# Row maxima as rows of the q stack, sent on ScalarE's DMA queue, and z transposed a step ahead, in a cross-attention block

## What is computed

```python
x = layer_norm(hidden_states, ln1_w, ln1_b)
q = (x @ q_w + q_b).reshape(B, LQ, H, HD).transpose(0, 2, 1, 3)
k = (encoder_hidden_states @ k_w + k_b).reshape(B, LK, H, HD).transpose(0, 2, 1, 3)
v = (encoder_hidden_states @ v_w + v_b).reshape(B, LK, H, HD).transpose(0, 2, 1, 3)
scores = jnp.einsum('bhqd,bhkd->bhqk', q, k) * scale
scores = jnp.where(mask, scores, mask_value)
attn = jax.nn.softmax(scores, axis=-1)
out = jnp.einsum('bhqk,bhkd->bhqd', attn, v).transpose(0, 2, 1, 3).reshape(B, LQ, D)
hidden = out @ cproj_w + cproj_b + hidden_states
y = layer_norm(hidden, ln2_w, ln2_b)
return hidden + jax.nn.gelu(y @ fc_w + fc_b, approximate=True) @ proj_w + proj_b
```

## Time and profile before

| | |
|---|---|
| median of 3 runs | 260.66 us |
| profiled execution | 260.52 us, span 258.70 us |
| TensorE busy (matmul) | 229.5 us, 89% of the span |
| VectorE, ScalarE, GpSimd busy | 184.1, 124.5, 92.9 us |
| chain that ended last | 72% TensorE, 15% VectorE, 6% issue, 4% DMA |
| granted TensorE clock, mean | 0.914 |
| DMA | 22.9 MB, all from SP's queue, 48.2% of the 16 engines' time |

### The profile page before, as it was taken

One profiled execution on the slowest core, in us unless ns is written; L12 is line 12 of the kernel. 1 busy time (PEld: TensorE's weight loads), 2 busy tenths in 40 slices (PEclk: granted clock), 3 DMA queues, 4 the chain that ended last, 5 costly groups with the idle time before them and its releaser, 6 DMA issues.

```text
span 258.7 us, 8205 instructions
## 1 busy us (share of the span) xinstructions
PE 229.5 (89%) x3452; PEld 210.5 (81%) x3452; DVE 184.1 (71%) x379; ACT 124.5 (48%) x269; POOL 92.9 (36%) x104
## 2 busy tenths in 40 slices
PE   0596849967999999899999999999999998799795
PEld 0495838956999899798889899989898997699695
DVE  2998974586369957894689579957994598349661
ACT  3335645223672496149723873387339724442050
POOL 6639532023352156215430644164315311112300
PEclk9959765595799999999999999999999999689999
DMA  6898994003650079309940792089408930100011
GB/s 216 263 291 163 129 178 68 1 5 67 106 117 4 1 184 152 38 4 175 150 47 3 167 169 38 1 167 156 51 3 138 119 34 4 43 0 3 3 41 41
DMA packets 23494, 22.89 MB, mean 88 GB/s; under 512 B 2337, under 2 KB 23201, under 8 KB 23458
## 3 DMA queue, kind: packets, MB, share of 16 engines
q1 hardware_dynamic: 23458, 22.37, 48.2%
HBM read 7.62 MB, written 2.10 MB: 38 GB/s over the span
## 4 chain that ended last, share of the span: by engine, by line
PE 72%; DVE 15%; issue 6%; DMA 4%; ACT 1%; POOL 1%; SPq 0%; ACTq 0%; POOLq 0%; DVEq 0%
PE bank L1026 18%; PE bank L1028 15%; PE bank L1027 15%; PE bank L1101 7%; PE scores L1085 5%; PE scores L1078 4%; PE scores L1056 3%; PE bank L1043 3%; DMA k_stack<-mask_row 2%; DVE recip L821 2%; DVE z L863 1%; DVE g_hi L838 1%; DVE mx L776 1%; PE bank L1164 1%; DMA w_raw_k<-in_k_w 1%
## 5 line engine op out<-in xcount | busy, mean ns | idle before, releaser
L821 DVE RECIPROCAL recip<-bank 128x256 f32<-128x256 f32 x16 | 28.1, 1757 | 22.1 <-PE bank L1101 22.1
L1026 PE MATMUL bank<-z_hi,fc_hi 128*128 128x256 f32 x128 | 38.5, 301 | 0.0
L1026 PE MATMUL bank<-proj_hi,g_hi 128*128 128x256 f32 x128 | 37.3, 291 | 1.0 <-DVE g_lo L840 0.9
L1028 PE MATMUL bank<-z_lo,fc_hi 128*128 128x256 f32 x128 | 36.2, 283 | 0.0
L1027 PE MATMUL bank<-z_hi,fc_lo 128*128 128x256 f32 x128 | 36.2, 283 | 0.0
L1027 PE MATMUL bank<-proj_hi,g_lo 128*128 128x256 f32 x128 | 35.7, 279 | 0.0
L1028 PE MATMUL bank<-proj_lo,g_hi 128*128 128x256 f32 x128 | 35.7, 279 | 0.0
L565 POOL TENSOR_TENSOR o_lo<-o,o_hi 128x256 fp32r<-128x256 f32 x16 | 16.6, 1038 | 40.3 <-ACT o_hi L609 40.3
L616 ACT ACTIVATE fc_raw<-bank,fc_bias 128x256 f32<-128x256 f32 x64 | 26.4, 466 | 5.7 <-PE bank L1028 5.7
L552 POOL TENSOR_TENSOR rs<-ve,power 128x1 f32<-128x1 f32 x16 | 9.0, 566 | 53.7 <-DVE ve L801 53.7
L1026 PEld LDWEIGHTS bank<-z_hi,fc_hi 128*128 128x128 f32 x128 | 24.5, 192 | 1.6
(11 more groups left out here) (114 smaller groups left out, 621.4 us busy)
## 6 DMA issues: line engine op xcount, KB each, us to landing
k_stack<-part_k SPq DMA_DIRECT2D x48, 128.0 KB, 4.4
q_stack<-part_q SPq DMA_DIRECT2D x48, 128.0 KB, 5.5
ctx_in<-in_ctx_t SPq DMA_DIRECT2D x8, 256.0 KB, 5.5
x_in<-in_x SPq DMA_DIRECT2D x8, 256.0 KB, 3.4
out<-y SPq DMA_DIRECT2D x7, 256.0 KB, 2.2
fc_raw<-in_fc_w SPq DMA_DIRECT2D x1, 1024.0 KB, 8.6
proj_raw<-in_proj_w SPq DMA_DIRECT2D x1, 1024.0 KB, 10.9
w_raw_k<-in_k_w SPq DMA_DIRECT2D x1, 256.0 KB, 3.3
```

Source lines behind the costliest of these rows:

```text
L821: ve.reciprocal(recip[:], bank7[:, 1, :, :]).then_inc(recip_made, 1)
L1026: mm(out_ap, a_hi, b_hi, start=first, stop=False, skip_group_check=True)
L1028: return mm(out_ap, a_hi, b_lo, start=False, stop=last, skip_group_check=True)
```

## The change

Three things are changed.

1. The maxima's parts become two more rows of q_stack, behind the mask row (SCORE_ROWS = 97, SHIFT_ROWS = 99), with ones in the same rows of k_stack. After keep_maxima, ScalarE's own DMA queue copies n_t[p] (32 rows of 128) to these two rows for all 16 heads: 32 pieces of 256 B, stack_maxima, with a semaphore per half (n_stacked). shift then needs no select products; its 16 + 16 products read 99 rows, those of score 97. n_parts is written in the order of head_pos, interleaved. select and what built it on GpSimd are gone, and n_t is free again when its copy has landed.
2. z is normalized, transposed and split one step ahead: turn_z of the next group stands between MLP chunks 2 and 3, high_of_z at the end of ScalarE's step, normal1 between the two outputs on VectorE, rest_of_z in its old place behind maxima(a, 1). make_q(a) then follows k directly, behind turn_maxima(b, 1).
3. SP issues both loads of the next group first, then the mask row and the parts of k and q in turn: lead k, lead q, second k, second q, third k, third q. The other engines' lists follow: lead_q and second_q come earlier on ScalarE, keep_v later, third_q earlier on GpSimd; on VectorE left_k stands between the two halves of normal2, left_q ahead of rest_of_z2, maxima(a, 0) ahead of part 2 and part 3 behind hidden(b, 0).

The diff, cut to its core:

```diff
+SCORE_ROWS = MASK_ROW + 1
+SHIFT_ROWS = SCORE_ROWS + N_PARTS
...
-        select = sb("select", [N_PARTS * H, HP, 2, S], BF16)
...
             def full_step(a, b, c, ahead=True):
 
                 if ahead:
                     load_x(Group(a.j, a.c + 1))
+                    load_ctx(Group(a.j, a.c + 1))
                 sp.wait_ge(shifted, a.count(4, -4))
                 stack_mask(a)
-                stack_k(a)
-                if ahead:
-                    load_ctx(Group(a.j, a.c + 1))
-                stack_q(a)
+                stack_k(a, (0,))
+                stack_q(a, (0,))
+                for k in (1, 2):
+                    stack_k(a, (k,))
+                    stack_q(a, (k,))
                 store(c)
...
             def keep_maxima(g, p):
                 act.wait_ge(n_turned, g.count(2, p + 1))
-                wait(act, shifted, g.count(4, 2 * p - 2))
+                wait(act, n_stacked[p], g.count(16))
                 sc.copy(n_t[p][:], n_t_ps).then_inc(n_kept, 1)
+
+            def stack_maxima(g, p):
+
+                act.wait_ge(n_kept, g.count(2, p + 1))
+                act.dma_start(q_stack[g.slot][SCORE_ROWS:SHIFT_ROWS, :, P * p:P * p + P], n_t[p][:]) \
+                   .then_inc(n_stacked[p], 16)
...
             def shift(g, p):
 
                 q, k = q_stack[g.slot], k_stack[g.slot]
-                pe.wait_ge(n_kept, g.count(2, p + 1))
+                pe.wait_ge(n_stacked[p], g.count(16, 16))
...
                 for s in range(2):
                     for i in range(4):
-                        mm(scores[:, s, P * i:P * i + P], select[:, 4 * s + i, :, :].rearrange("r w k -> r (w k)"),
-                           n_t[p][:], start=(i == 0), stop=False, skip_group_check=True)
-                    for i in range(4):
                         for b in range(2):
...
                                 last = mm(scores[S * par:S * par + S, s, P * i + S * b:P * i + S * b + S],
-                                          k[:, pos, rows], q[:, pos, rows], start=False, stop=True,
+                                          k[0:SHIFT_ROWS, pos, rows], q[0:SHIFT_ROWS, pos, rows],
+                                          start=True, stop=True,
                                           skip_group_check=True)
...
                 turn_maxima(b, 1)
-                turn_z(a)
+                make_q(a)
                 shift(b, 0)
                 make_v(a, 0)
...
-                make_q(a)
                 shift(b, 1)
...
-                mlp_chunks(c, (2, 3)).then_inc(mlp_made, 1)
+                mlp_chunks(c, (2,))
+                if ahead:
+                    turn_z(Group(a.j, a.c + 1))
+                mlp_chunks(c, (3,)).then_inc(mlp_made, 1)
```

More of the change, by code:

```diff
@@ L718, in full_step @@
                 keep_maxima(b, 1)
-                high_of_z(a)
+                lead_q(a)
+                stack_maxima(b, 1)
+                exp(b, 0)
                 second_k(a)
-                exp(b, 0)
                 high_of_z2(c)
-                keep_v(a)
-                lead_q(a)
+                second_q(a)
                 exp(b, 1)
```

83 lines of the change are left out of this document (44 added, 39 removed).

## The result

The changed kernel takes 259.23 us in the median of 20 runs (256.14 to 262.11), the kernel before, beside it, 260.70 us (20 runs, 259.45 to 263.34). The ratio is 0.9926, 95% interval 0.9899 to 0.9953: 0.7% faster, less than the 1% that the prediction set as its bound, and not the 252.2 us forecast. 259.23 lies outside the range of 248.3 to 258.0.

A forecast was written before the change was run, and what follows sets the result against it. TensorE's list of products was taken to bound a full step (25.56 us plus idle pieces, 26.23 mean). Terms of -1.1, -1.0, -4.5, -1.3, +0.35 and -0.8 sum to -8.35: 260.52 to 252.2 us, range 248.3 to 258.0 (8 in 10).

The forecast's parts named there:

- second step and up to u: Low clock, up to the first full u (end of turn_maxima(b, 1)): shifts shed 2.15 us, turn_z eats half, -1.1 us.
- first full step: First full step, half at low clock: -1.74 - 1.05 + 0.64 + 0.2 + 0.55 + 0.4 = -1.0 us.
- four full steps: Four full steps of 24.5 + 0.4 + 0.2 = 25.1 us against 26.23: -4.5 us.
- last full step: Last full step up to 207.3: -1.30 - 0.59 + 0.2 + 0.4 = -1.3 us.
- TensorE's list: TensorE's products in a full step: without selection products, uninterrupted time falls from 25.56 to 24.5 us.
- The copy of the maxima: Ahead of shift(b, 1): copy leaves at u + 2.0, lands 2.8 us later, TensorE waits 0.4 us (0 to 1.4).
- rival C: Maxima's copy caught in DMA traffic: 264.2 to 272.7 us, deciding from 4.2 us landing; chance 0.10, half mild (257 to 263).
- The late landing of the earlier trace goes away: Stacks ahead of first_score: q's start some 3 us earlier, copies end by u + 12, first_score comes at about u + 17.
- rival D: Stacks still land last: first_score waits about 0.6 us a step, 255.8 us; chance 0.10.
- 0.2 a step: TensorE's unexplained 0.71 us idle piece in the full steps, kept in the forecast at 0.2 us a step.
- over 7 us: Maxima's copy for p = 0: shift(b, 0) needs it over 7 us after the maxima are kept, so it is covered.
- Rival B: ScalarE pays for the DMA instruction ahead of exp(b, 0): 0.6 us more per full step, 255.8 us; chance 0.15.

The follow-up runs named there:

- e12: Changed kernel without the maxima's copies and with four of the twelve stack copies of each full step cut to 8 KB: 251.98 us, ratio 0.9657 to the kernel before.
- e16: The changed kernel itself, unedited, run once more: 258.74 us, ratio 0.9922 to the kernel before.
- e3: Changed kernel without the copies of the maxima, so no maximum is subtracted: 256.02 us, ratio 0.9797 to the kernel before.
- e2: Changed kernel with the second half's maxima copy issued ahead of lead_q instead of behind it: 258.84 us, ratio 0.9976 to the kernel before.
- e14: Changed kernel with first_score one MLP chunk later and VectorE's parts of chunk 2 ahead of the maxima: 258.53 us, ratio 0.9962 to the kernel before.
- e15: Changed kernel with first_score one MLP chunk later and the maxima's copy ahead of lead_q: 257.25 us, ratio 0.9871 to the kernel before.
- e17: Changed kernel with first_score one chunk later, maxima's copy ahead of lead_q, VectorE's parts of chunk 3 ahead of hidden(b, 0): 256.25 us, ratio 0.9744.
- e11: Kernel before with four of the twelve stack copies of each full step cut to 8 KB: 258.16 us, ratio 0.9851 to the kernel before.
- e18: The kernel before, unchanged, run once more with its own profile: 261.18 us, ratio 1.0006.
- p1: Kernel before with only the maxima's rows and their copies replacing the selection products, all in the old order: 260.24 us, ratio 0.9838.
- e4: Changed kernel with ctx's load moved behind the stacks' first parts, x's load left at the head: 265.53 us, ratio 1.0168 to the kernel before.
- e7: Changed kernel with the loads of x and ctx issued behind the stack copies, a step ahead: 262.72 us, ratio 1.0087 to the kernel before.
- e1: Changed kernel with the maxima's copy cut in two DMAs of one row each: 263.77 us, ratio 1.0068 to the kernel before.
- e10: Changed kernel, maxima's copies kept, with four of the twelve stack copies of each full step cut to 8 KB: 256.17 us, ratio 0.9812.
- e8: Changed kernel with both loads behind the stack copies and the maxima's copy ahead of lead_q: 262.43 us, ratio 1.0140 to the kernel before.
- e13: Changed kernel with the six q stack copies issued on ScalarE's queue in the full steps: 276.95 us, ratio 1.0578 to the kernel before.

## Why the prediction was wrong

By parts, as differences from the kernel before in the two profiled executions (us):

| | forecast | measured |
|---|---|---|
| second step and up to u | -1.1 | +2.4 |
| first full step | -1.0 | -2.3 |
| four full steps | -4.5 | -1.5 |
| last full step | -1.3 | 0.0 |
| behind it | -0.45 | -0.5 |

In the four full steps of the changed kernel TensorE is idle 5.75 us: 3.81 for the copy of the maxima, 1.18 for the stacks, 0.45 ahead of a product of weigh, 0.31 for z_lo. The forecast had 2.4 in all.

**TensorE's list: right.** Forecast 24.5 us uninterrupted; e12's best steps take 24.57 and 24.63 with 0.31 of waiting in each (for z_lo in front of fc_chunk(c, 0), which starts at u + 5.22; forecast u + 5.15 without the copy). The shift was one group of 0.70 us (0.74 forecast), and the rows of 97 and 99 cost nothing visible.

**The copy of the maxima: the step that failed first, by its size.** It left at u + 1.65, sooner than the 2.0 I took, and landed 3.7 to 4.1 us later (3.5 to 4.8 in e16) instead of 2.8: waits of 1.06, 1.31, 0 and 1.44 us in the four steps, mean 0.95, where "Wait: 0.4 us" stood. The row that I sized it by was the wrong one. The mask row's copy came behind the store and one load in the kernel before, this one meets the store, x and ctx; in the changed kernel the mask row's own copy, issued at 116.50 and 168.07, landed after 3.36 and 3.85 us. In the two steps without a wait the copy was there within 2.6 us: at 141.9, where SP's instruction for x's load took 1.28 us so that the loads came late, and at 194.0, where there are no loads. This is rival C in its mild form. By itself it does not make the miss: 0.95 instead of 0.4 in six steps is 3.3 us by the prediction's own sum (an estimate), 255.5 and inside the range, and in this profile the landing stayed under the 4.2 us from which rival C was to decide.

**"The late landing of the earlier trace rows goes away": the step that failed behind it.** I wrote that first_score comes at about u + 17 and that the copies are issued by u + 12. They are, nearly (at u + 12.3 in the step with u at 114.27). But u + 17 is where TensorE stood in the kernel before (106.06, u + 17.2); with the shorter list of this change it is there at u + 15.6, and the stacks land between u + 16.3 and 17.1 (e3). The prediction shortened the list and left this time as it was. That is rival D; forecast at 0.6 us a step and 10% as a thing by itself, measured at 1.04 (e3: 5.2 us in five steps). I took C and D for alternatives; they are two waits in a row, of which the first hides part of the second. e2 and e14 show it from both sides: moving one of them alone gives no gain (258.84 and 258.53 us against 258.74 of e16). e15, which moves both, has steps of 25.45 us where e16 has 26.19 and the first trace of the changed kernel 25.85; its median is 1.5 us lower, e17's 2.5, of which only the second is clear of noise. e12, without the copy and with a third of the bytes gone, has the list as forecast and comes to the forecast time.

**The kernel before waited for the stacks already.** I took its 26.23 us as list plus unexplained idle, "0.2 a step" of which I carried over. In e11 the 0.7 us a step beyond the list are gone with a third of the stacks' bytes. Two of the three idle pieces of the earlier trace rows's steps stand ahead of first_score (1.03 us up to 107.09, 0.44 up to 185.35), and each ends 0.09 us behind the landing of the last q copy, which was issued at 100.38 and 179.24 (first the chain, then that copy alone, for the first of the two):

```profile
106.06 1.03 issue
107.09 0.88 PE scores L1056 x32
...
L340 SPq DMA_DIRECT2D q_stack<-part_q x1: 588/588/588, 100.4 to 100.4; - x1
DMA to landing us min/median/max: 6.6/6.6/6.6
```

So the wait had been in the trace before the change: the prediction set the landing (107.2) beside first_score (107.1) and carried nothing of it over. The third piece, 0.71 us, stands ahead of a product of weigh, which reads no stack. It is gone in e11 too, but it came in one step of four only; here, in e18 and in the changed kernel such pieces end 1.6 to 1.8 us behind a packet of 16 KB on the DMA queue that the profile calls "instruction" (126.29 to 127.98 ahead of 129.81), and whether TensorE waited for its own instructions there no run tests.

Where the stacks' landing is the bound, a gain of 1.2 us in the list can bring only what the new order brings the stacks forward. That the order does this is shown by p1 and e4, which have the shorter list without it or without the load's place, and pay 1.80 to 3.85 us at once.

**The second step.** Forecast -1.1. From the end of turn_maxima(b, 0) to u it took 23.95 us (23.89 in e16) against 23.32 and 23.23 in the two profiles of before: +0.7. The missing piece is the copy for p = 0. I covered it by "over 7 us", which holds in the full steps; in the second step TensorE was there 4 us after its issue at 38.58 and waited 2.12 us (up to 44.66 above; 1.95 in e16, and 2.2 less without the copy: 21.76 us in e3). In the five microseconds between, the 16 engines are full and not one packet of ScalarE's queue (q10) has gone; only SP's queue (q1) moves, with stack copies and the two loads. The queues (packets, MB, share of the 16 engines) in the window 38.5:43.7 and, behind the second row of dots, in 43.7:44.6:

```profile
DMA packets 926, 0.87 MB, mean 168 GB/s; under 512 B 74, under 2 KB 926, under 8 KB 926
...
q1 hardware_dynamic: 926, 0.87, 115.1%
...
q1 hardware_dynamic: 80, 0.07, 21.9%
q10 hardware_dynamic: 68, 0.02, 8.2%
```

With one load less in the way (p1, e4) this wait is 0.26 and 0.20 us. The other +1.8 us up to there lie before the change does anything and vary by as much between traces of one kernel (e18), so they are no effect.

**First and last steps.** The first full step fell by 2.3 us instead of 1.0, at a granted clock of 0.94 in place of 0.86; it took 28.06 us in e18 and 26.24 in e16 (29.04 and 26.74 in the first profiles), and what part of that is the change is not settled. The last full step did not gain (24.12 us, forecast about 1 less): it waited 0.87 us for the stacks at 208.85, and without that, in e12, it took 23.16.

**Rival B: no.** exp(b, 0) starts at u + 2.4 with one DMA instruction ahead of it, as in the kernel before (117.94 in the earlier trace rows, u + 2.25).

## What to carry to other kernels

When a wait is priced by the nearest row, match the traffic around it and not only the shape: a copy of 8 KB landed within 2.6 us where no load stood ahead, in 3.5 to 4.8 among a store and two loads, and 6.1 us after its issue among stack copies and two loads (the second step). Before an engine's list is shortened, ask for every transfer that its list waits for how long it has been there already, with the new time at which the engine comes: where an idle "without a releaser" ends with the landing of such a transfer, the next microsecond saved will be waited for there. And where two landings follow each other in one list, take both away in one experiment before either is judged: here moving one alone gained nothing in time (e2, e14), and leaving the first out gained 0.1 us in a full step between the two profiles (e3).

## What the runs showed of the hardware

**A long wait costs TensorE more than its length.** In e2 the wait of 2.13 us ahead of first_score at 105.8 is followed by a stretch at the lower of the two clock levels (granted clock 0.50, that is 1.2 GHz), shown by these windows (the last three columns are clock, DMA share and GB/s):

```profile
103.70:105.80 2.10, 0.00 (x0) 0.01 (x1) 0.00 (x0) 0.00 (x0) 0.42 (x1) 1.00 0.15 19
105.80:107.00 1.20, 1.18 (x35) 1.16 (x36) 0.45 (x1) 0.00 (x0) 0.00 (x0) 0.85 0.00 0
107.00:109.00 2.00, 2.00 (x11) 2.00 (x11) 1.90 (x5) 0.00 (x0) 0.00 (x0) 0.50 0.03 8
109.00:111.00 2.00, 2.00 (x41) 1.80 (x39) 1.85 (x8) 0.26 (x1) 0.46 (x1) 0.74 0.01 4
```

That step is busy 25.71 us where the next one with the same instructions is busy 24.31: the wait cost 2.13 + 1.4 us. Some 1.2 to 1.5 us of extra busy time stood in e7's steps with waits of 2.28 and 2.70 us, in e16's with 2.14 (the step of 28.00), and in e1's with 1.96; p1's wait of 3.67 cost 2.6 more. No wait up to 1.50 us in the full steps of these profiles did so by itself; of those between 1.5 and 1.8 us some did (1.54 in e4, 1.66 in e10, 1.80 in p1) and some did not (1.65 in e12, 1.71 in e1). The forecasts counted each wait once, so e4 and e7 had to come out worse than any sum of waits. It may also be what spreads the runs, since one late landing is worth 3.5 us.

**The rate of SBUF copies on busy engines is not one number.** The stacks' 1.57 MB a step ran at about 120 to 165 GB/s with the same DMA share of 1.1 to 1.2, by step and by kernel; the lower end is the rule where no load has gone ahead (e7, e8, the last full steps). What sets it is open.

**DMA instructions on ScalarE's queue** took 0.62 us each and ran beside an activation already begun; further ones in a row held the next activation (0.43 us behind two in e1, 2.10 behind four in e13).
